# A decoder block on one core: GpSimd does the query norm's power before the four weight splits of a slot

## The chip, the cores and the metric

The kernel runs on one NeuronCore of a Trainium2 chip. The metric is the device time of one execution in microseconds (us); lower is better. TensorE (PE) multiplies, VectorE (DVE), ScalarE (ACT) and GpSimd (POOL) do the elementwise work, and SyncE's queue (SP) issues every DMA.

## The reference, cut to what matters

A decoder block over 32 sequences of 64 tokens with 512 features, in float32:

```
x = x + self_attention(layernorm(x))        # 32 heads of 16, 8 key-value heads, causal
x = x + cross_attention(layernorm(x), ctx)  # 32 heads of 128, 8 key-value heads; queries and keys RMS-normed
x = x + ffn(layernorm(x))                   # squared ReLU, a latent path, a final layernorm

# cross attention, where the change is:
q = rmsnorm(hidden @ Wq.T) ; k = rmsnorm(ctx @ Wk.T) ; v = ctx @ Wv.T
rmsnorm(t, w) = t * rsqrt(mean(t * t) + 1e-5) * w
out = softmax(q @ k.T / sqrt(128)) @ v ; return out @ Wo.T
```

## The kernel before, in words

The batch is done in two halves of 1024 tokens. Each half goes through self attention, cross attention and the feed-forward part. Every large product is done as three matmuls in a rounded float type (`split_mm`), so each operand exists twice: a rounded part (`_hi`) and the rest (`_lo`). ScalarE makes the `hi` part by a copy that rounds, and GpSimd or VectorE makes the `lo` part by a subtraction.

Cross attention takes one key-value head with its four query heads at a time, called a group; there are 8. A group's weights are six pieces. The loop `Fori(0, NG - 1)` runs 7 turns in each half, 14 in all; a turn works on one group and brings in the pieces of the next, numbered 6 to 11 in the code (6 and 7: keys and values, 128x512; 8 and 9: queries; 10 and 11: output; these four 128x1024). A piece passes through four stations:

- SP loads it into one of three places of `stage` (`load_piece`, L286 is its DMA). The load of piece n waits until `w_lo_done` has counted the split of piece n - 3, so the load of 9 waits for GpSimd's split of 6, that of 10 for 7, that of 11 for 8.
- ScalarE makes `w_hi` (`split_piece` of ScalarE, L686), once the piece has landed.
- GpSimd makes `w_lo = stage - w_hi` (`split_piece` of GpSimd, L1265), once `w_hi` is there, and this frees the place in `stage`.
- TensorE waits for both (`pieces_split`) at the first use in the next group.

Each turn has four slots, one for each chunk of 256 tokens (`slot(place, k)`, k = 0 to 3). In slot k the engines work on three chunks at once: the projections and norms of chunk k + 2 ("front"), the scores and softmax of chunk k + 1 ("mid"), the output projection of chunk k ("back"). TensorE's order in a slot is: keys and values of k + 2 (L342 to L344 with 256 columns), scores (L526), queries of k + 2, an output tile, transposes of the probabilities (L383), an output tile, values (L540), and last `transpose_chunk`: eight transposes of the queries (L360) and two of the keys (L511). Those eight wait until VectorE has scaled both queries and keys.

Each engine runs its instructions in the order in which they are written. Around the change, in slot 1:

- VectorE: `variance` (L1067, writes `qkve`), an update of x (L1005), `scale_chunk` (L1074 scales the queries, 128x1024; L1077 the keys, 128x256; only L1077 counts `qk_nrm`, which TensorE waits for), a second update, then `outputs_lo` (L946). L1074 waits for GpSimd's power.
- GpSimd: `subtract_max` (L1278), `normalise_probs` (L1284), then in the order that the change alters `split_piece` and `norm_rsqrt` (the power, L1269).
- ScalarE: in slot 1 its copy of the output (L813) is followed by its split of piece 9, and that by the evacuation of the chunk's transposes (`transposed_chunk`, L802 twice and L807). It reads:

```
if mid:
    outputs_hi(at, k + 1)
if next_group and k == 1:
    split_piece(place, 9)
if front:
    transposed_chunk(at, k + 2)
```

TensorE's transposes of the keys (L511) need the accumulator that the first L802 frees, and the next slot's keys and values need the one that the second frees.

Of the kernel before, what the change touches and what calls it, by code (L numbers as in the profile page):

```python
# [66 lines left out]
class Place:  # L67
# [5 lines left out]
    def at(self, c, k):  # L73

        value = c.n0 + k
        if self.stage > 1:
            value += c.n1
        if self.stage > 2:
            value += NG * c.n2
        value = self.half * (c.by * (c.n1 + NG * c.n2 + c.n3)) + c.by * value  # L80
        if self.stage == 2 and c.n2:
            value = self.turn * (c.by * c.n2) + value
        return value
# [14 lines left out]
def decoder_block(nc, x_in, ctx_in, mask_in, w_self, w_cross, qn_in, kn_in, w_ffn,  # L98
                  f1g_in, expt_in, fc2_in, gamma_in, beta_in, out):
    with ExitStack() as stack:  # L100
# [155 lines left out]
        def spread(small, count_, width):  # L256

            return small.unsqueeze(2).to_broadcast([P, count_, width])
# [1000 lines left out]
        def _(pool):  # L1259
            def split_piece(place, n):  # L1260

                pool.wait_ge(w_hi_done, place.piece(n)[1] + 1)
                high, width = piece_target(place.stage, n, 0)
                low, _ = piece_target(place.stage, n, 1)
                nc.gpsimd.tensor_tensor(low, stage[:, place.slot(n), 0:width], high.bitcast(F32), ALU.subtract  # L1265
                                        ).then_inc(w_lo_done, 1)

            def rsqrt(target, source, width):
                return nc.gpsimd.tensor_tensor(target, source, mhalf[:, 0:width], ALU.pow)  # L1269
# [5 lines left out]
            def subtract_max(at, u, buffer):  # L1275
                pool.wait_ge(s_max.sem, at(s_max, u + 1))
                pr = prob[:, buffer, :].rearrange("p (g k) -> p g k", g=8)
                nc.gpsimd.tensor_tensor(pr, pr, spread(pmax[:, buffer, :], 8, SEQ), ALU.subtract  # L1278
                                        ).then_inc(s_sub.sem, 1)

            def normalise_probs(at, u, buffer):
                pool.wait_ge(s_rec.sem, at(s_rec, u + 1))
                pr = prob[:, buffer, :].rearrange("p (g k) -> p g k", g=8)
                nc.gpsimd.tensor_tensor(pr, pr, spread(prec[:, buffer, :], 8, SEQ), ALU.mult).then_inc(s_nrm.sem, 1)  # L1284
# [47 lines left out]
            def norm_rsqrt(at, k):  # L1332
                pool.wait_ge(qk_ve.sem, at(qk_ve, k + 1))
                rsqrt(qkrs[:, k % 2, :], qkve[:, k % 2, :], 2 * REP + 2).then_inc(qk_rs.sem, 1)

            def slot(place, k, front=True, mid=True, next_group=True):
                at = place.at
                if mid:
                    subtract_max(at, k + 1, (k + 1) % PRING)
                    normalise_probs(at, k + 1, (k + 1) % PRING)  # L1340
                if next_group and k == 1:
                    split_piece(place, 6)
                    split_piece(place, 7)
                if front:
                    norm_rsqrt(at, k + 2)
                if next_group and k == 1:
                    split_piece(place, 8)
                    split_piece(place, 9)
                if next_group and k == 3:
                    split_piece(place, 10)  # L1350
                    split_piece(place, 11)

            def cross_attention(half):
                place = Place(2, half, 0)
                split_piece(place, 4)
                split_piece(place, 5)
                slot(place, -2, mid=False)
                slot(place, -1)
                with pool.Fori(0, NG - 1) as turn:
                    for c in range(CHUNKS):  # L1360
                        slot(Place(2, half, turn), c)
# [101 lines left out]
```

## Time and profile before

| what | value |
|---|---|
| median of 3 runs | 1974.14 us (1969.96 to 1976.91) |
| profiled execution, own time | 1979.39 us |
| its span | 1977.7 us |
| PE busy | 1769.2 us, 89% of the span |
| DVE busy | 939.0 us, 47% |
| ACT busy | 748.8 us, 38% |
| POOL busy | 720.3 us, 36% |
| DMA queue | 70.05 MB, 11.3% of the 16 engines' span |
| granted TensorE clock, mean | 0.946 |
| PE's share of the chain that ended last | 82% |

All start times below count from the start of the span. The granted clock is a share of full speed: 1.00 is 2.4 GHz and 0.50 is 1.2 GHz. In a timeline row the square bracket is the time that the engine sat idle before the row's first instruction, and what released it. Where a row holds several instructions ("x2"), its duration is that of all of them. An instruction that waits for something inside the engine shows as a longer one, not as idle time.

### The profile page before, as it was taken

The numbers are of one execution on the slowest core, as the hardware profiler recorded it, in microseconds if no ns is written. First come the engines' busy times: TensorE is split into PE (matmuls) and PEld (weight loads), VectorE is DVE, ScalarE is ACT, GpSimd is POOL, SyncE is SP. The second block draws the span as 40 slices with busy tenths as digits, with TensorE's granted clock in tenths as the row PEclk, the third lists the DMA queues.
The fourth block names the chain that finished last, engine by engine and source line by source line (L and its number), as shares of the span: only waits on it lengthen the run. The fifth ranks groups of instructions, "written<-read, shape, count | busy, mean of one in ns | idle before, by whom it ended". The sixth has DMA issues, their size and how long they took to land.

```text
span 1977.7 us, 29620 instructions
## 1 busy us (share of the span) xinstructions
PE 1769.2 (89%) x11352; PEld 1421.5 (72%) x11352; DVE 939.0 (47%) x1629; ACT 748.8 (38%) x1332; POOL 720.3 (36%) x539
## 2 busy tenths in 40 slices
PE   3888689999999999989959887899999999999898
PEld 1745477777787777778936555787877777777787
DVE  3167434444444444474451764444444444445744
ACT  2365333434433433431223653433334344344311
POOL 2186313433433334261022762333334234334410
PEclk7889789999999999999958997999999999999999
DMA  4010001101101101010041100101011011011100
GB/s 153 29 38 17 17 1 38 53 16 37 48 21 37 32 26 53 22 54 17 17 139 31 33 6 17 33 22 37 16 37 53 16 37 53 16 42 33 44 22 22
DMA packets 25872, 70.92 MB, mean 36 GB/s; under 512 B 3153, under 2 KB 3153, under 8 KB 25809
## 3 DMA queue, kind: packets, MB, share of 16 engines
q1 hardware_dynamic: 25808, 70.05, 11.3%
q8 instruction: 43, 0.70, 0.1%
q14 instruction: 21, 0.16, 0.0%
HBM read 65.85 MB, written 4.19 MB: 35 GB/s over the span
## 4 chain that ended last, share of the span: by engine, by line
PE 82%; ACT 6%; issue 5%; DVE 3%; POOL 2%; DMA 2%; SPq 0%; ACTq 0%; POOLq 0%; DVEq 0%
PE acc L342 14%; PE acc L344 12%; PE acc L343 12%; PE y L342 9%; PE y L344 8%; PE y L343 8%; PE acc L360 4%; PE sc L526 4%; PE ot L540 3%; PE sc L449 2%; ACT qb L802 2%; PE pt L383 2%; DMA kv<-in_ctx 1%; PE sc L447 1%; ACT w_hi L686 1%
## 5 line engine op out<-in xcount | busy, mean ns | idle before, releaser
L1265 POOL TENSOR_TENSOR w_lo<-stage,w_hi 128x1024 fp32r<-128x1024 f32 (+1 forms) x116 | 242.6, 2106 | 236.2 <-ACT w_hi L686 236.2
L1278 POOL TENSOR_TENSOR prob<-prob,pmax 128x512 f32<-128x512 f32 x128 | 133.7, 1045 | 500.9 <-DVE pmax L988 500.0
L342 PE MATMUL y<-w_hi 128*128 128x512 f32 x576 | 236.9, 411 | 28.0 <-issue 24.5
L342 PE MATMUL acc<-w_hi,xn_hi 128*128 128x512 f32 (+1 forms) x576 | 227.7, 395 | 2.9 <-DVE xn_lo L946 2.9
L344 PE MATMUL y<-w_hi,w_lo 128*128 128x512 f32 x576 | 229.8, 399 | 0.0
L343 PE MATMUL y<-w_lo,w_hi 128*128 128x512 f32 x576 | 228.7, 397 | 0.0
L344 PE MATMUL acc<-w_hi,xn_lo 128*128 128x512 f32 (+1 forms) x576 | 220.5, 383 | 0.0
L343 PE MATMUL acc<-w_lo,xn_hi 128*128 128x512 f32 (+1 forms) x576 | 219.5, 381 | 0.0
L1284 POOL TENSOR_TENSOR prob<-prob,prec 128x512 f32<-128x512 f32 x128 | 142.0, 1109 | 108.1 <-DVE prec L996 108.1
L982 DVE TENSOR_TENSOR prob<-sc,mask 128x512 f32<-128x512 f32 x64 | 44.3, 692 | 283.7 <-PE sc L526 283.7
L1269 POOL TENSOR_TENSOR qkrs<-qkve,mhalf 128x10 f32<-128x10 f32 x64 | 125.0, 1953 | 126.5 <-DVE qkve L1067 124.8
L342 PE MATMUL acc<-w_hi,cx_hi 128*128 128x256 f32 x512 | 159.2, 311 | 4.6 <-DVE xn_lo L946 0.9
L694 ACT ACTIVATE prob<-prob 128x512 f32<-128x512 f32 x128 | 81.0, 633 | 197.2 <-POOL prob L1278 196.9
L343 PE MATMUL acc<-w_lo,cx_hi 128*128 128x256 f32 x512 | 151.7, 296 | 0.0
L344 PE MATMUL acc<-w_hi,cx_lo 128*128 128x256 f32 x512 | 151.0, 295 | 0.0
L1061 DVE TENSOR_REDUCE qkss<-kbd 128x4 f32<-128x512 f32 x128 | 87.8, 686 | 127.7 <-ACT kbd L796 124.8
L342 PEld LDWEIGHTS y<-w_hi 128*128 128x128 f32 x576 | 110.5, 192 | 52.4 <-issue 28.4
L813 ACT CAST w_hi<-ot 128x1024 fp32r<-128x1024 f32 x64 | 64.8, 1012 | 187.9 <-PE ot L540 187.9
L993 DVE TENSOR_REDUCE psum_<-prob 128x8 f32<-128x512 f32 x128 | 87.2, 681 | 100.8 <-ACT prob L694 100.7
L1005 DVE TENSOR_TENSOR x<-y,x 128x512 f32<-128x512 f32 x144 | 98.8, 686 | 66.1 <-PE y L344 64.2
L342 PEld LDWEIGHTS acc<-w_hi,xn_hi 128*128 128x128 f32 x576 | 110.5, 192 | 25.5 <-issue 3.6
L344 PEld LDWEIGHTS y<-w_hi,w_lo 128*128 128x128 f32 x576 | 110.6, 192 | 24.9
(127 smaller groups left out, 3792.1 us busy)
## 6 DMA issues: line engine op xcount, KB each, us to landing
stage<-in_w_cross SPq DMA_DIRECT2D x64, 512.0 KB, 3.6
stage<-in_w_cross SPq DMA_DIRECT2D x32, 256.0 KB, 2.7
stage<-in_w_ffn SPq DMA_DIRECT2D x16, 512.0 KB, 3.5
kv<-in_ctx SPq DMA_DIRECT2D x16, 256.0 KB, 3.7
x<-in_x SPq DMA_DIRECT2D x8, 512.0 KB, 6.7
stage<-in_w_self SPq DMA_DIRECT2D x8, 512.0 KB, 4.0
out_x<-x SPq DMA_DIRECT2D x16, 256.0 KB, 2.0
stage<-in_w_self SPq DMA_DIRECT2D x4, 256.0 KB, 7.4
```

What stands on the lines that cost most here:

```text
L342: nc.tensor.matmul(target, l_hi, r_hi, start=first, stop=False)
L343: nc.tensor.matmul(target, l_hi, r_lo, start=False, stop=False)
L344: return nc.tensor.matmul(target, l_lo, r_hi, start=False, stop=last)
L360: ins = nc.tensor.transpose(to[:, k * P:(k + 1) * P], source[:, k * P:(k + 1) * P], ident[:])
L694: nc.scalar.activation(prob[:, buffer, :], prob[:, buffer, :], ACT.Exp).then_inc(s_exp.sem, 1)
L993: nc.vector.tensor_reduce(psum_[:, buffer, :], prob[:, buffer, :].rearrange("p (g k) -> p g k", g=8), AX_X, ALU.add).then_inc(s_sum.sem, 1)
L1005: nc.vector.tensor_tensor(x[:, i % NT, :], y[i % 2][:], x[:, i % NT, :], ALU.add).then_inc(y_free.sem, 1)
L1061: nc.vector.tensor_reduce(qkss[:, k % 2, t * REP:(t + 1) * REP], qsq[:, t], AX_X, ALU.add).then_inc(q_sum.sem, 1)
L1265: nc.gpsimd.tensor_tensor(low, stage[:, place.slot(n), 0:width], high.bitcast(F32), ALU.subtract).then_inc(w_lo_done, 1)
L1269: return nc.gpsimd.tensor_tensor(target, source, mhalf[:, 0:width], ALU.pow)
L1278: nc.gpsimd.tensor_tensor(pr, pr, spread(pmax[:, buffer, :], 8, SEQ), ALU.subtract).then_inc(s_sub.sem, 1)
L1284: nc.gpsimd.tensor_tensor(pr, pr, spread(prec[:, buffer, :], 8, SEQ), ALU.mult).then_inc(s_nrm.sem, 1)
```

## The change

In the slot with k = 1 GpSimd used to split pieces 6 and 7, do the power, and split pieces 8 and 9. Now it does the power first and then splits 6, 7, 8 and 9. The same instructions are issued; in the other slots nothing is different.

```diff
@@ -1338,12 +1338,11 @@
                 if mid:
                     subtract_max(at, k + 1, (k + 1) % PRING)
                     normalise_probs(at, k + 1, (k + 1) % PRING)
+                if front:
+                    norm_rsqrt(at, k + 2)
                 if next_group and k == 1:
                     split_piece(place, 6)
                     split_piece(place, 7)
-                if front:
-                    norm_rsqrt(at, k + 2)
-                if next_group and k == 1:
                     split_piece(place, 8)
                     split_piece(place, 9)
                 if next_group and k == 3:
```

## Rows read from the trace of the kernel before

**Rows 1.** The chain that ended last: start us, us, what; two turns.

```profile
370.37 1.08 PE sc L526 x32
...
391.85 1.08 PE sc L526 x32
...
448.99 1.08 PE sc L526 x32
...
468.98 1.08 PE sc L526 x32
...
488.03 1.08 PE sc L526 x32
```

**Rows 2.** Timeline of POOL, slot 1 of one turn: start us, us, line, operation.

```profile
455.36 2.54 POOL L1265 TENSOR_TENSOR w_lo<-stage,w_hi 128x512 fp32r<-128x512 f32 x2
458.03 1.95 POOL L1269 TENSOR_TENSOR qkrs<-qkve,mhalf 128x10 f32<-128x10 f32 x1
460.56 2.89 POOL L1265 TENSOR_TENSOR w_lo<-stage,w_hi 128x1024 fp32r<-128x1024 f32 x1 [0.58 <-ACT w_hi L686]
464.90 2.38 POOL L1265 TENSOR_TENSOR w_lo<-stage,w_hi 128x1024 fp32r<-128x1024 f32 x1 [1.45 <-ACT w_hi L686]
```

**Rows 3.** Timeline of DVE, the same slot.

```profile
457.78 0.17 DVE L1067 TENSOR_SCALAR qkve<-qkss 128x10 f32<-128x10 f32 x1
...
460.01 1.23 DVE L1074 TENSOR_TENSOR qb<-qb,qkrs 128x1024 f32<-128x1024 f32 x1 [0.81 <-POOL qkrs L1269]
461.15 2.58 DVE L1077 TENSOR_TENSOR kv<-kv,qkrs 128x256 f32<-128x256 f32 x1
```

**Rows 4.** All L1077 of the program: ns min/median/max, first and last start.

```profile
L1077 DVE TENSOR_TENSOR kv<-kv,qkrs x64: 418/420/2590, 246.4 to 1826.9; 128x256 f32<-128x256 f32 x64
```

**Rows 5.** Timeline of PE, end of slot 1 and start of slot 2.

```profile
461.61 1.13 PE L540 MATMUL ot<-probt,kv 64*128 64x256 f32 x8
463.79 1.09 PE L360 MATMUL acc<-ident,qb 128*128 128x128 f32 x8 [1.04 <-DVE kv L1077]
465.37 0.44 PE L511 MATMUL acc<-ident,kv 128*128 128x128 f32 x2 [0.48 <-ACT qb L802]
465.85 0.39 PE L342 MATMUL acc<-w_hi,cx_hi 128*128 128x256 f32 x1
```

**Rows 6.** Timeline of ACT, the same stretch.

```profile
463.78 1.05 ACT L686 CAST w_hi<-stage 128x1024 fp32r<-128x1024 f32 x1
464.73 1.07 ACT L802 COPY qb<-acc 128x512 f32<-128x512 f32 x2
```

**Rows 7.** SP's timeline in slot 1; issue to landing of all loads into `stage`.

```profile
456.81 10.98 SPq L286 DMA_DIRECT2D stage<-in_w_cross  x4
...
DMA to landing us min/median/max: 2.5/3.6/7.7
```

**Rows 8.** Timelines of POOL and DVE in the feed-forward part.

```profile
904.92 0.55 POOL L1269 TENSOR_TENSOR yrs<-yve,mhalf 128x1 f32<-128x1 f32 x1 [12.44 <-DVE yve L1168]
905.43 1.29 POOL L1391 TENSOR_TENSOR x<-x,beta 128x512 f32<-128x512 f32 x1
...
905.55 1.71 DVE L1177 SCALAR_TENSOR_TENSOR x<-qb,yrs,x 128x512 f32<-128x512 f32 x1
...
971.51 0.75 DVE L1177 SCALAR_TENSOR_TENSOR x<-qb,yrs,x 128x512 f32<-128x512 f32 x1
```

**Rows 9.** Timelines of DVE and POOL in self attention.

```profile
119.85 1.02 DVE L1034 TENSOR_TENSOR kbd<-kt,gsel 128x512 f32<-128x512 f32 x1
...
120.28 1.49 POOL L1284 TENSOR_TENSOR prob<-prob,prec 128x512 f32<-128x512 f32 x1
```

**Rows 10.** Windows: busy us by engine, then clock, DMA share, GB/s.

```profile
308.50:313.20 4.70, 4.65 (x27) 4.46 (x26) 0.00 (x0) 0.53 (x2) 1.52 (x1) 0.64 0.36 123
...
465.80:468.90 3.10, 3.05 (x25) 2.93 (x24) 0.00 (x0) 0.48 (x1) 1.48 (x1) 1.00 0.29 101
```

**Rows 11.** Timeline of PE in a slot that fills the pipeline, ahead of a loop.

```profile
265.69 1.97 PE L360 MATMUL acc<-ident,qb 128*128 128x128 f32 x8 [3.02 <-DVE kv L1077]
```

## The prediction

> **What bounds the kernel now.** I read the page first: PE is busy for 89% of the span and holds 82% of the chain that ended last, so what counts is whether PE waits longer or shorter. Then the chain in order of time. In cross attention it passes the scores (L526) once in a slot, which gives each slot's length [rows 1]. A plain slot takes 488.03 - 468.98 = 19.05 us. Slot 1 of that turn, the only one that the diff touches, takes 468.98 - 448.99 = 19.99 us, and that of an earlier turn 391.85 - 370.37 = 21.48 us. I read this difference in all 14 turns: slot 1 took about 21.5 us in six of them and 20.0 us in eight. So slot 1 costs 0.94 us over a plain slot in every turn, and 1.49 us more in six.
>
> Where the 0.94 us come from stands in the timelines of the slot. PE ends the values (L540) at 462.74 and waits 1.04 us for L1077 [rows 5]. L1077 is drawn as 2.58 us [rows 3], where its median is 0.42 us [rows 4]. It is stuck until GpSimd's split of piece 8 ends at 460.56 + 2.89 = 463.45, and ends 0.28 us behind it at 463.73 [rows 2, 3]. That split is itself 0.51 us longer than the split of piece 9 (2.38 us), because it first waited for L1074, which ended at 461.24. So these two scalings, which read both inputs from SBUF, and a GpSimd split don't run together: one stands until the other is over. Each hands over to the other side when it ends.
>
> The 1.49 us are the clock. In the six turns PE runs the next keys and values at a granted clock of 0.64 over that stretch, partly at 1.2 GHz, in the others at 1.00, which is 2.4 GHz [rows 10]. Ahead of it stands the stretch from 462.74 to 465.85 in which PE has only ten transposes to do [rows 5]; both kinds of turn have that stretch, and six of 14 lose the clock after it.
>
> **The power is not started earlier.** Its input `qkve` is written by 457.78 + 0.17 = 457.95, and the power starts at 458.03, 0.08 us later and 0.13 us after the split of 7 has ended at 457.90 [rows 2, 3]. In the slots without splits it starts at the same distance from `qkve`, 0.07 to 0.08 us. So pieces 6 and 7 are split today in a hole in which GpSimd would have to wait anyway. I take 0 us gained; the most that it could be is those 0.13 us, which only pull L1074 forward. With the new order GpSimd idles from 455.39 to 458.03, does the power until 459.98, and pieces 6, 7 and 8 come behind it.
>
> **Who gets the way first at 459.98.** Split 6 has all it needs and follows the power directly; L1074 has to see the power's signal. In the feed-forward part the same situation is there: the power ends at 905.47, GpSimd's next instruction starts at 905.43, the VectorE instruction that waited for the power at 905.55, and that one takes 1.71 us instead of 0.75 us [rows 8]. It lost, and ended 0.54 us after GpSimd's (906.72). So I take split 6 first: from 459.95 for 1.25 to 1.27 us (half of 2.54) to 461.21.
>
> The Trainium skill states the same lock (SBUF — State Buffer, section Who interferes with whom: whoever issues first has the shared pair for the whole instruction). The rows above agree with it, 1.71 against 0.75 us. By its rule, were L1074 the first to issue, the order would be that of rival A, and the sum 14 x 2.35 instead of 14 x 1.25 us. It doesn't say who is next when both sides queue.
>
> For that I have a row: VectorE's L1034 came in while GpSimd had instructions back to back; it ended at 120.87, and the GpSimd instruction that stood next was 0.45 us longer (1.49 against its usual 1.04) [rows 9]. The side that waits gets its turn. So behind split 6 comes L1074, until 461.21 + 1.08 = 462.3; then split 7, about 462.1 to 463.4; then L1077, which ends some 0.28 us behind it as today, at 463.7; then split 8, 463.5 to 465.9; then split 9. Today L1077 ends at 463.73. The transposes (L360) start where they do now: the scalings stand behind two short splits instead of one long one. Term: 0 us, within 0.1 either way.
>
> **What comes late: the load of piece 9.** SP issues it 0.18 us after split 6 has ended: split 6 ended about 456.63, the issue is at 456.81 [rows 2, 7]. It lands 3.6 us later, at 460.4, which is the median of all loads into `stage` [rows 7], and ScalarE needs it at 463.78 [rows 6]: a cover of 3.4 us. With split 6 ending at 461.21 the issue is at 461.38, 4.6 us later, and the landing at 464.98. The least of all is 2.5 us, and the longest ones, up to 7.7 us [rows 7], share the DMA engines with other loads, which this one doesn't.
>
> ScalarE's order puts the evacuation of the transposes (L802) behind its split of piece 9. That split starts at about 465.03 instead of 463.78, 1.25 us late. The first L802 goes from 464.73 to 465.98. PE's L511 starts 0.64 us after the first L802 [rows 5, 6], so at 466.62 instead of 465.37, and the next keys and values at 467.10 instead of 465.85. PE has nothing else to do there, and a stall in slot 1 is passed on in full (today's wait of 1.04 us shows as 0.94 us). Term: 14 x 1.25 = **17.5 us**. Bounds: with a landing of 3.3 us 0.95 x 14 = 13.3; with 3.9 us 21.7.
>
> **The other queues.** The loads of 10 (behind split 7, 463.4) and 11 (behind split 8, 465.9) are wanted in slot 3, some 30 us on: 0 us. PE needs `lo` of 6 and 7 at 467.1: they are there at 461.2 and 463.4; if that cover of 3.7 us were gone, PE would wait by the excess. Split 9 runs from about 466.1, when ScalarE has made its `hi`, to 468.4; PE wants it for the queries, 4.1 us after the keys and values start, at 471.2; GpSimd's `subtract_max` comes after that as well. Their cover is 2.8 us. On VectorE L1005 and L946 stand behind L1077 and start as now. SP has no other load in these stretches.
>
> **The clock.** The stretch with little work for PE grows from 3.1 to 4.4 us, and its idle part from 1.6 to 2.8 us. In the four slots that fill the pipeline (246.84, 265.69, 1222.28, 1241.48) PE idles for 3.0 to 5.8 us in one piece ahead of L360; each time the transposes then run at half speed, 1.97 us for eight instead of 1.09 us [rows 5, 11]. So it is 6 of 14 at 1.6 us idle and 4 of 4 at 3.0 us or more. Between them I take 12 of 14: 6 more x 1.49 = **8.9 us**. Bounds: none more (0), all of them (8 x 1.49 = 11.9).
>
> **The sum.** 17.5 + 8.9 = 26.4 us over the profiled execution's own 1979.39 us (its span 1977.7 us plus 1.7 around it) gives 2005.8 us. That execution is 5.3 us above the median. The runs spread over 7 us; if that is the clock (9.4 us from 1979.39 to 1969.96 is about six losses of 1.49 us), the median run has some three losses fewer, and has more to lose after the change, which comes to 2006 too; if it is the profiler, the sum is 1974.14 + 26.4 = 2000.5. I take 2004 us.
>
> **Rivals.** My forecast, split 6 first and ScalarE late by some 1.25 us: chance 0.74, its own range 14 x 0.95 with no more clock losses to 14 x 1.55 with 8 more, on 1974 to 1979: 1988 to 2013 us.
>
> A: L1074 gets the way first. Then split 6 ends at about 462.3, the load of 9 lands at 466.1, ScalarE is 2.35 us late, although L1077 is done by 462.6. For it: L1074 starts only 0.03 us behind the power's end. Against it: rows 8, in which the same race went to GpSimd each time that it had an instruction ready. 14 x 2.35 = 33 us and up to 12 us of clock on 1974 to 1979: 2015 to 2024 us. Chance 0.13.
>
> B, the other side: the scalings come free of the splits, and the load makes no wait. PE then starts the transposes at 462.74; the 0.94 us are gained 14 times (13.2 us) and the six clock losses with it (8.9 us): 1952 us. It decides at one point: the load of 9 must have landed by 463.78, so it may take 2.4 us from an issue at 461.38, where 3.6 us were measured and 2.5 us was the least, for half the bytes. And L1077 would have to pass splits 6 and 7. Chance 0.04.
>
> C: ScalarE is late by less than 0.4 us, because split 6 gets done in the hole before the power after all, or the load comes at 2.8 us, and the clock stays as it is: 1974 to 1980 us, no change that can be told. Chance 0.04. The rest, 0.05, is slower than A: losses of clock that last longer than today's.
>
> **How the numbers follow.** 0.3% of the time is 6 us, about what a measurement of this kernel can tell from no change. Slower by more: the forecast, A and the rest, 0.92, less 0.02 for mild ends of the forecast: 0.90. Within: C and those ends, 0.06. Faster: B, 0.04. The range 1990 to 2018 us leaves out B, C, half of A and the slowest rest, and thin ends of the forecast.
>
> **What the profile of the changed kernel would show.** In slot 1: the power's start 0.08 us behind L1067 with an idle bracket; split 6 right behind it; L1074 longer than 1.23 us (about 2.3) and L1077 about 1.5 instead of 2.58; PE's L360 starting as today; ScalarE's split of 9 with a wait for a DMA in front, and L511 waiting 1.7 us for L802 instead of 0.48; slot 1 at 21.2 us or, with the clock lost, 22.7. The prediction is wrong if the load lands in time, if L1074 isn't blocked, or if the clock is lost in six turns as before.

## The result and the profile after

The changed kernel takes 2001.19 us, median of 6 runs (1994.38 to 2003.75), against 1972.35 us before (6 runs, 1968.67 to 1976.91): a ratio of 1.0139, with a 95% interval of 1.0117 to 1.0161. The forecast was 2004 us, 1990 to 2018. The profiled execution took 2000.67 us, its span is 1998.9 us, 21.2 more than the span before.

The first look goes to the slot in the same turn. This is PE's timeline of the changed kernel at the end of slot 1, the counterpart of [rows 5]:

```profile
462.50 1.14 PE L540 MATMUL ot<-probt,kv 64*128 64x256 f32 x8
464.66 1.09 PE L360 MATMUL acc<-ident,qb 128*128 128x128 f32 x8 [1.02 <-DVE kv L1077]
467.50 0.44 PE L511 MATMUL acc<-ident,kv 128*128 128x128 f32 x2 [1.75 <-ACT qb L802]
471.05 1.15 PE L526 MATMUL sc<-kt,qb 128*64 128x64 f32 x32
```

The transposes of the queries wait as long as before (1.02 us for L1077), and they start 2.16 us behind the start of the values, before 2.18. The transposes of the keys wait 1.75 us instead of 0.48. In this turn, which kept its clock, all of the loss is in this second bracket. What it hangs on is in ScalarE's timeline, against [rows 6]:

```profile
463.75 1.01 ACT L813 CAST w_hi<-ot 128x1024 fp32r<-128x1024 f32 x1 [2.38 <-PE ot L540]
465.91 1.05 ACT L686 CAST w_hi<-stage 128x1024 fp32r<-128x1024 f32 x1 [1.15 <-DMA stage<-in_w_cross]
466.87 1.06 ACT L802 COPY qb<-acc 128x512 f32<-128x512 f32 x2
```

A bracket with a DMA in it stands in front of the split of piece 9, where before there was none; L802 follows behind the split. The cause one station further back is in the timelines of GpSimd and SP, against [rows 2, 7]:

```profile
458.91 1.95 POOL L1269 TENSOR_TENSOR qkrs<-qkve,mhalf 128x10 f32<-128x10 f32 x1 [2.62 <-DVE qkve L1067]
460.82 6.00 POOL L1265 TENSOR_TENSOR w_lo<-stage,w_hi 128x512 fp32r<-128x512 f32 x3
...
462.28 7.64 SPq L286 DMA_DIRECT2D stage<-in_w_cross  x4
```

The power idles 2.62 us for its input, splits 6 to 8 come behind it in one row of 6.00 us, and SP issues the first load at 462.28. This turn begins 0.88 us later than before (scores at 449.80 against 448.92), so the issue is 4.6 us late. VectorE's row shows the two scalings, against [rows 3]:

```profile
460.89 2.31 DVE L1074 TENSOR_TENSOR qb<-qb,qkrs 128x1024 f32<-128x1024 f32 x1 [0.80 <-POOL qkrs L1269]
463.12 1.48 DVE L1077 TENSOR_TENSOR kv<-kv,qkrs 128x256 f32<-128x256 f32 x1
```

L1074 waited for split 6 and L1077 for split 7. L1077 ends at the same place in the slot as before: 464.60 here is 463.72 when the 0.88 us are taken off, against 463.73.

Over the program, ScalarE's and PE's waits in the changed kernel read (us in total, times, longest):

```profile
ACT w_hi L686 <- DMA stage<-in_w_cross: 15.1, 14, 1.1
...
PE acc L511 <- ACT qb L802: 55.3, 60, 1.8
```

The DMA wait is new and comes once in each of the 14 turns. PE's wait for L802 was 38.4 us in total before, so it grew by 16.9 us.

I measured slot 1 from scores to scores in all 14 turns. Before it was 20.0 us in eight and 21.5 us in six. After, it is 21.06 to 21.25 us, mean 21.16, in seven, and 22.3 to 23.6 us in the other seven. The windows of one of each kind, in the changed kernel, tell them apart by the granted clock (span, then busy us of PE, PEld, DVE, ACT and POOL, clock, DMA share, GB/s):

```profile
449.80:471.05 21.25, 18.43 (x128) 15.02 (x127) 10.27 (x13) 9.63 (x16) 12.38 (x7) 1.00 0.28 76
606.58:630.14 23.56, 20.82 (x127) 17.35 (x126) 10.27 (x13) 9.63 (x16) 12.36 (x7) 0.86 0.27 78
```

The seven slower slots are 12.4 us above 21.16 us in sum; the six of before were 8.9 us above 20.0. So the 21.2 us between the two profiled spans are 14 x (21.16 - 20.00) = 16.3 us of wait, 12.4 - 8.9 = 3.5 us of clock, and 1.4 us outside these slots. Each count of slots here and below is from one profiled execution, and the number of losses differs between executions of one kernel, as the section on the prediction shows.

### The profile page after: what moved, and what is told of

Its sections match the earlier page's. It is cut to its first block, busy times and chain, and to the rows that moved or that the text cites. A ratio compares the mean times of both kernels' runs of the same rounds, so it can differ in the third digit from the quotient of the medians.

```text
span 1998.9 us, 29620 instructions
## 1 busy us (share of the span) xinstructions
PE 1773.9 (89%) x11352; PEld 1427.0 (71%) x11352; DVE 937.2 (47%) x1629; ACT 750.4 (38%) x1332; POOL 728.3 (36%) x539
## 4 chain that ended last, share of the span: by engine, by line
PE 73%; issue 9%; ACT 5%; POOL 5%; DMA 4%; DVE 4%; SPq 0%; POOLq 0%; ACTq 0%; DVEq 0%
PE acc L342 12%; PE acc L344 11%; PE acc L343 11%; PE y L342 7%; PE y L344 7%; PE y L343 7%; PE acc L360 4%; PE sc L526 4%; PE ot L540 3%; DMA stage<-in_w_cross 3%; ACT qb L802 2%; PE sc L449 2%; PE pt L383 2%; POOL prob L1278 1%; POOL prob L1284 1%
## 5 line engine op out<-in xcount | busy, mean ns | idle before, releaser
L1265 POOL TENSOR_TENSOR w_lo<-stage,w_hi 128x1024 fp32r<-128x1024 f32 (+1 forms) x116 | 250.9, 2180 | 209.7 <-ACT w_hi L686 209.4
```

## The experiments

Two questions were open. The first is whether the load of piece 9 is the cause, or the scalings that stand behind the splits. The second is about my reading of the kernel before: slot 1 is 0.94 us longer than a plain slot, and I put that down to the stuck L1077.

**Undo the consequence, keep the change (e1).** ScalarE's order in slot 1 of the changed kernel:

```diff
-                if next_group and k == 1:
-                    split_piece(place, 9)
                 if front:
                     transposed_chunk(at, k + 2)
+                if next_group and k == 1:
+                    split_piece(place, 9)
```

> The changed kernel with one more move: in slot 1 ScalarE does the evacuation of the transposes (L802, L807) first and its split of piece 9 behind it. Theory (the wait for the load of 9 stands in front of the evacuation): L511 no longer waits for the load, slot 1 falls from 21.2 to about 19.6 us, 14 times, and the time from 2001 to 1965 to 1978 us, at or below the kernel before. Rival (the scalings stuck behind splits 6 and 7 cost the time): L1074 is still 2.3 us and L1077 1.5 us, and the time stays at 1997 to 2003 us. Rival (only the lost clock): it falls by at most 12 us, to about 1989.

It took 1962.49 us (1961.01 to 1965.61); against the kernel before on the same chip the ratio is 0.994 (0.9927 to 0.9954). GpSimd's order is that of the changed kernel, and L1074 and L1077 still reach 2310 and 1486 ns. PE in slot 1:

```profile
455.90 1.14 PE L540 MATMUL ot<-probt,kv 64*128 64x256 f32 x8
458.06 1.09 PE L360 MATMUL acc<-ident,qb 128*128 128x128 f32 x8 [1.03 <-DVE kv L1077]
459.39 0.44 PE L511 MATMUL acc<-ident,kv 128*128 128x128 f32 x2 [0.24 <-ACT qb L802]
```

The first bracket is unchanged and the second is down from 1.75 to 0.24 us. Slot 1 takes 19.66 to 19.76 us in all 14 turns, none of them with a lost clock. So the loss sits in ScalarE's evacuation (L802), which stood behind its split of 9, and not in the blocked scalings. The time is 2.5 us below the range that was expected (1965 to 1978 us), though slot 1 was put nearly right. The 14 slots together are 32.7 us shorter than in the changed kernel, and the profiled spans differ by 39.6 us; the other 6.9 us lie where the code is the same, and I haven't traced them.

**The same move on the kernel before (e2).** The same edit, on the other base.

> The kernel before with ScalarE's split of piece 9 behind the evacuation. If slot 1 costs its 0.94 us over a plain slot because L1077 is stuck behind the split of 8 (as the prediction read it), the transposes still start 1.04 us late and this changes slot 1 by 0.1 us or less. If ScalarE's split of 9 in front of L802 is the later of the two, L511 comes some 0.35 us earlier: slot 1 at about 19.6 us, 1962 to 1970 us with the clock.

It took 1963.59 us (1960.41 to 1968.19), ratio 0.994 (0.9924 to 0.9956), the same as e1 beside it. With ScalarE's order mended, GpSimd's order makes no difference that can be measured. Slot 1 is 19.73 to 19.75 us in all 14 turns, 0.25 us less than the 20.0 us before, and no turn loses the clock. This is the second of the two readings: in the kernel before ScalarE's split of 9 is the later of the two that hold up the end of slot 1, and L1077 would end it 0.25 us earlier.

**Free the scalings (e4).** GpSimd in slot 1 of the kernel before:

```diff
                 if next_group and k == 1:
+                    pool.wait_ge(qk_nrm.sem, at(qk_nrm, k + 3))
                     split_piece(place, 8)
                     split_piece(place, 9)
```

> The kernel before, in which GpSimd waits for the end of the scalings (qk_nrm) before its split of piece 8, so that L1077 is not stuck (0.42 us instead of 2.58). If the stuck L1077 costs the 0.94 us of slot 1, the time falls by 14 x 0.94 = 13 us and by up to 9 us of clock more: 1950 to 1960 us. If ScalarE's split of 9, which stands in front of L802, sets the end, L802 starts at the same time as before, only the place of the idle time changes, and the time stays within 1968 to 1977 us.

It did what it should: L1077 is at most 421 ns in the whole program. PE then shows:

```profile
460.38 1.14 PE L540 MATMUL ot<-probt,kv 64*128 64x256 f32 x8
461.44 1.09 PE L360 MATMUL acc<-ident,qb 128*128 128x128 f32 x8
464.13 0.44 PE L511 MATMUL acc<-ident,kv 128*128 128x128 f32 x2 [1.59 <-ACT qb L802]
```

The transposes start at once, and the whole wait reappears one instruction later. Slot 1 is 19.99 to 20.00 us in the four turns at full clock, exactly as before, and 21.4 to 21.5 us in the other ten. The time is 1986.28 us (1982.03 to 1989.66), ratio 1.0058 (1.0042 to 1.0074): slower, and above both ranges that were expected. The slot came out as the second reading had it, but not the clock. The profiled execution has ten losses where that of before has six, 5.8 us more in these slots, and is 3.2 us shorter in the rest, where the code is the same. The granted clock says the same of all runs: its mean is 0.939 to 0.943 in the six runs of e4 and 0.945 to 0.950 in the eleven of the kernel before beside them. Slot 1 at 20.0 us without the stuck L1077 says that my reading of the 0.94 us was wrong; why the clock is lost more often isn't shown.

**Both moves (e6).**

> Both moves on the kernel before: GpSimd waits for the scalings before the split of 8, ScalarE does its split of 9 behind the evacuation. Either reading: slot 1 like a plain slot, 19.05 us, 14 x 0.94 = 13 us gained and the clock not lost there (up to 9 us): 1950 to 1960 us. If the split of 9 then comes too late for the next group's queries, PE waits there instead, and it is 1960 us or more.

It took 1951.03 us (1947.23 to 1955.75), ratio 0.9886 (0.987 to 0.9902). Chain of this kernel, scores (L526), start us and us:

```profile
442.20 1.08 PE sc L526 x32
461.25 1.08 PE sc L526 x32
480.30 1.08 PE sc L526 x32
```

The first interval is slot 1, the second a plain one, and both are 19.05 us; so it is in all 14 turns, and none loses the clock. This is the fastest version: 1.1% below the kernel before (the ratio above) and 2.5% below the changed one (1951.03 / 2001.19, medians from two sets of runs). e1 and e2 are 0.6% below the kernel before.

**The power ahead of one split only (e3).** The kernel before, in the order 6, power, 7, 8, 9:

```diff
                     split_piece(place, 6)
-                    split_piece(place, 7)
                 if front:
                     norm_rsqrt(at, k + 2)
                 if next_group and k == 1:
+                    split_piece(place, 7)
                     split_piece(place, 8)
```

> The kernel before with the power moved ahead of one split only: 6, power, 7, 8, 9. The load of 9 is issued as early as before. Load theory with the lock: L1074 waits for split 7, L1077 for split 8 (2.4 us), ends about 1.05 us later than before, and L511 comes 0.7 us later: slot 1 at 20.7 us, 1980 to 1992 us with the clock. Load theory alone: as before, 1968 to 1977 us. If it is the power's place ahead of the splits that costs, whatever the load does, most of the 29 us should be there: 1990 us or more.

It took 1990.89 us (1988.93 to 1993.53), ratio 1.0084 (1.0066 to 1.0101). The load of 9 is in time here: ScalarE never waits for it. VectorE's scalings in slot 1, and what PE does behind them:

```profile
460.45 2.29 DVE L1074 TENSOR_TENSOR qb<-qb,qkrs 128x1024 f32<-128x1024 f32 x1 [0.81 <-POOL qkrs L1269]
462.68 2.57 DVE L1077 TENSOR_TENSOR kv<-kv,qkrs 128x256 f32<-128x256 f32 x1
...
465.30 1.97 PE L360 MATMUL acc<-ident,qb 128*128 128x128 f32 x8 [2.10 <-DVE kv L1077]
```

L1074 waits for split 7, L1077 for split 8, the long one, and the transposes wait 2.10 us instead of 1.04. (This is a turn in which the clock is lost already at the transposes: eight take 1.97 us instead of 1.09.) Slot 1 at full clock is 20.75 to 20.82 us, 0.77 more than before (0.7 expected), but only in three turns; eleven lose the clock, at 1.1 us or more each. The time alone would fit the last reading as well (1990 us or more, the power's place costs whatever the load does); the slot at full clock, 20.77 us against the 20.7 of the lock and the 21.16 of the changed kernel, and L1077 at 2.57 us speak for the lock. So the handover by turns that the forecast relied on holds, and the lock does cost time where a long split stands last. The changed kernel escapes that: there the two scalings wait for the two short splits.

**Only the load, later (e5).** The kernel before, GpSimd's order untouched:

```diff
+                if place.stage == 2 and place.turn is not None and n == 9:
+                    sp.wait_ge(w_lo_done, number - SRING + 3)
-                if first >= SRING:
+                elif first >= SRING:
                     sp.wait_ge(w_lo_done, number - SRING + 1)
```

> The kernel before, GpSimd's order untouched; only SP issues the load of piece 9 later, behind the split of 8 instead of 6, 6.8 us later. Load theory: the cover is 3.4 us, so ScalarE is late by 3.4 us in each of 14 turns: 48 us and up to 20 us of clock, 2020 to 2045 us. Rival (the load is hidden, the scalings cost): 1968 to 1977 us.

It took 2035.16 us (2031.97 to 2038.35), ratio 1.0312 (1.0291 to 1.0333), in the middle of what was expected. ScalarE and PE (this kernel has two more lines, so L686 is L688 and L511 is L513):

```profile
474.17 1.04 ACT L688 CAST w_hi<-stage 128x1024 fp32r<-128x1024 f32 x1 [3.42 <-DMA stage<-in_w_cross]
...
475.76 0.67 PE L513 MATMUL acc<-ident,kv 128*128 128x128 f32 x2 [4.01 <-ACT qb L804]
```

The wait of 3.42 us is the one that the cover predicts (6.8 - 3.4). All 14 turns lost the clock as well, with slots of 24.7 to 25.1 us.

**The load a little later (e7).** The same edit with `+ 2` in place of `+ 3`.

> The kernel before; SP issues the load of piece 9 behind the split of 7 instead of 6, 1.3 to 1.5 us later, which is within the cover of 3.4 us. Load theory: no change, 1968 to 1977 us. If any lateness of the load costs, 14 x 1.4 = 20 us: 1992 us.

It took 1973.97 us (12 runs, 1970.76 to 1976.61), ratio 1.0003 (0.9992 to 1.0014). Slot 1 is 20.0 us in 12 turns and 21.5 us in two. SP issues the load 1.3 us later than before, and in the turn that starts at 445.66 it lands 1.95 us before ScalarE needs it (458.57 against 460.52). A load that is late within its cover costs nothing that can be measured here. Its profiled execution, with two clock losses, took 1970.76 us and was the fastest of its 12; that of the kernel before, with six, took 1979.39 us. Of these 8.6 us four losses are 6.

## Why the prediction was right

**The power is not started earlier**: right. It starts behind an idle bracket of 2.62 us, as in a slot without splits.

**Who gets the way first**: right. L1074 was put at about 2.3 us and is 2.31; L1077 at about 1.5 and is 1.48; the transposes wait 1.02 us as before. Rival A, L1074 first, would have shown as 1.23 us. e3 shows the same alternation with another pair of splits. The trace agrees with the rule of the Trainium skill (SBUF — State Buffer, section Who interferes with whom), by which whoever issues first has the shared pair for the whole instruction: split 6 started 0.07 us before L1074, which took 2.31 instead of 1.23 us.

**The load of piece 9**: right, and shown. The issue was put 4.6 us late and is 4.6 us late; ScalarE's split was put 1.25 us late and is: 465.91 against 463.78 + 0.88 = 464.66. One remark on the way there was wrong and did no harm: the load of 9 isn't alone, the load of 10 is issued before it has landed (458.05 against a landing at 460.38 before, 464.48 against 465.89 after). It took 3.6 us both times. Over 14 turns the slot at full clock grew by 1.16 us in the mean, 16.3 us where the term said 17.5. e5 and e7 give the same relation without touching GpSimd: ScalarE is not late when the load is issued 1.3 us later, is 3.4 us late at 6.8 us, and in this change 1.2 us late at 4.6 us. What was put at 0 stayed there: a plain slot takes 19.05 us in both kernels.

**The clock**: mis-sized. The term was 12 losses for 6 at 1.49 us, 8.9 us more. The profile of the changed kernel has 7 losses, but dearer ones, 1.2 to 2.4 us each, and 3.5 us more in sum. The step that failed is the interpolation between "6 of 14" and "4 of 4" by idle time alone. The two brackets in front of the transposes in slot 1 and the turns that lost the clock, one execution of each kernel:

| kernel | idle, us | losses of 14 |
|---|---|---|
| e6 | 0.65 | 0 |
| e1, e2 | 1.3 | 0 |
| before, e7 | 1.5 | 6, 2 |
| e4 | 1.6 | 10 |
| e3 | 2.3 | 11 |
| changed | 2.7 | 7 |
| e5 | 5.0 | 14 |

More idle time mostly goes with more losses, but the changed kernel has fewer than e3 and e4. What of the stretch decides isn't settled by these runs.

**The sum**: 26.4 us forecast; the profiled executions differ by 21.3 us, the medians by 28.8. The sum by itself stood at 2005.8 us for the profiled execution, which took 2000.67: the clock term was 5.4 us too large, the wait 1.2 too large, and 1.4 us outside the slots were not foreseen. The medians went the other way, because the profiled execution of before (1979.39 us) is above all six of its timed runs and that of the changed kernel is near the median of its own. The forecast weighed whether that is the clock or the profiler, and left it open. The record speaks for the clock: in the 28 runs of the kernel before beside the experiments the mean granted clock is 0.950 to 0.951 in those under 1971 us and 0.945 to 0.946 in those over 1978 us, and the profiled execution, with 0.946, fits among them. Of the 28.8 us between the medians, then, 16.3 are the wait, and for the other 12.5 the clock is the likely source; no profile of a median run of before splits them. So it is in part luck that 2004 came within 3 us of 2001: the clock term is too large by the profiles and, if all of the 12.5 us are clock, too small by the medians. Rival A's range should have started at 2007 us (1974 + 33), not 2015.

**What bounds the kernel now**: one step was wrong, though it didn't enter the sum. It put slot 1's 0.94 us down to the stuck L1077. e4 removes that and gains nothing; e2 moves ScalarE's split of 9 and gains 0.25 us; only both together gain the 0.94 us. ScalarE's split of 9 alone makes slot 1 0.94 us longer, L1077 alone makes it 0.70 us longer (19.75 against 19.05), and they overlap. PE's first bracket (1.04 us) was so near to the slot's excess (0.94 us) that I took it for the cause. For the same reason rival B was mispriced: in e4 the scalings are free and the load is in time, and slot 1 gained nothing.

## What to carry to other kernels

Before a step is moved behind another on an engine, list what it frees as well as what it feeds: here a buffer's release started a load, and that load's landing stood in front of unrelated work in a third engine's queue. Write down the cover of each such release (issue to use, less the transfer); here the cost was what the move took beyond it, and nothing within it. When two waits end near each other on the critical engine, remove one at a time and then both: either alone may give nothing. And prefer to place work that waits for a transfer behind the work that the critical engine waits for.

## What the runs showed of the hardware

VectorE's scalings, with both inputs in SBUF, and GpSimd's splits, which read SBUF, took turns, even when each engine had more queued: with splits of 1.27, 1.27 and 2.37 us in GpSimd's queue, L1074 stood behind the first and L1077 behind the second (2.31 and 1.48 us), and with one short and one long split left, behind those (2.29 and 2.57 us). The wait shows in these rows as a longer instruction and not as an idle bracket. When the power ended and both engines had an instruction that could start, GpSimd's came first: L1074 was the long one in all 14 turns of the changed kernel (2.30 to 2.31 us), and so was L1177 [rows 8] in all ten such cases of the feed-forward part of the kernel before (1.71 to 1.72 us instead of 0.75).

The granted clock fell to 0.50 (1.2 GHz) after a stretch in which PE was idle for no more than 1.04 us at a time (six of 14 turns before), with ten transposes in it, and after e4's, whose longest idle piece is 1.59 us, in ten of 14. It did not fall in e1 and e2, whose slot is only 0.25 to 0.35 us shorter than the one before.
